# Interleaving the two batches through three layer norms and a convolution

## What is computed

```python
def _layernorm(x, axis=-1, eps=1e-05):
    m = jnp.mean(x, axis=axis, keepdims=True)
    v = jnp.var(x, axis=axis, keepdims=True)
    return (x - m) / jnp.sqrt(v + eps)
...
# fourth sublayer, with Z = _layernorm(x)
y = Z + summary
mu = jnp.mean(y, axis=-1, keepdims=True)
var = jnp.mean((y - mu) ** 2, axis=-1, keepdims=True)
x = x + (y - mu) / jnp.sqrt(var + LN_EPS) * gamma + beta
# fifth sublayer, with x = _layernorm(x)
z = x @ W_mem
z = lax.conv_general_dilated(z, conv_k, window_strides=(1,), padding=[(CONV_W - 1, 0)], ...)   # CONV_W = 4, depthwise
q = (x @ W_q).reshape(b, l, KQ, H, M, 2)
...                                    # phases, running sums, queries, gates, an output projection
```

## Time and profile before

| | us |
|---|---|
| median of 3 runs | 438.44 |
| lowest and highest run | 437.74, 439.62 |
| the profiled execution, whole | 437.43 |
| span of its trace | 435.6 |
| PE busy in the span | 395.9 |
| DVE busy in the span | 302.9 |

### The profile page before, as it was taken

How to read it: one execution, slowest core, us unless ns; L and a number is a source line. 1 busy time by engine, 2 the same in 40 slices (tenths; PEclk the granted TensorE clock), 3 DMA queues, 4 the chain that set the end, 5 groups by cost and what they waited for, 6 DMA issues and landing times.

```text
span 435.6 us, 14368 instructions
## 1 busy us (share of the span) xinstructions
PE 395.9 (91%) x6033; PEld 330.5 (76%) x6033; DVE 302.9 (70%) x676; ACT 266.9 (61%) x552; POOL 215.3 (49%) x262
## 2 busy tenths in 40 slices
PE   6978999999999999789979977799889998999997
PEld 4656767777667777678979966577768878989996
DVE  6788989988888876558798877583896668222221
ACT  2557878888888889675545513530999235445441
POOL 2468657765567663333544630510199734444540
PEclk8989999999999999999999989999999999999999
DMA  4186732622311003520000080030000291000000
GB/s 154 30 299 220 227 123 71 221 89 78 103 38 31 29 15 102 227 89 2 0 2 2 1 320 13 10 124 2 1 2 2 78 391 71 2 1 2 0 2 24
DMA packets 10831, 34.77 MB, mean 80 GB/s; under 512 B 2192, under 2 KB 7312, under 8 KB 8976
## 3 DMA queue, kind: packets, MB, share of 16 engines
q1 hardware_dynamic: 10480, 33.08, 21.7%
q10 hardware_dynamic: 288, 0.79, 0.5%
HBM read 33.60 MB, written 0.26 MB: 78 GB/s over the span
## 4 chain that ended last, share of the span: by engine, by line
PE 63%; DVE 20%; POOL 6%; ACT 5%; issue 4%; DMA 1%; SPq 0%; DVEq 0%; POOLq 0%; ACTq 0%
PE ps L1599 9%; PE ps L1089 8%; PE ps L1554 8%; PE ps L1075 6%; PE ps L405 3%; PE ps L1586 3%; PE ps L1569 3%; PE ps L466 2%; PE ps L815 2%; PE ps L797 2%; PE ps L391 2%; PE ps L351 2%; PE ps L756 2%; PE ps L763 2%; ACT sb_arena L1520 1%
## 5 line engine op out<-in xcount | busy, mean ns | idle before, releaser
L1520 ACT ACTIVATE sb_arena<-ps 128x1024 f32<-128x1024 f32 x128 | 123.4, 1019 | 22.5 <-PE ps L1586 22.4
L1599 PE MATMUL ps<-sb_arena 128*25 128x128 f32 (+1 forms) x2048 | 69.0, 274 | 0.9 <-issue 0.8
L1599 PEld LDWEIGHTS ps<-sb_arena 128*25 128x25 f32 (+1 forms) x2048 | 50.4, 97 | 8.3 <-issue 1.2
L1554 PE MATMUL ps<-sb_halves 128*128 128x512 f32 x192 | 54.3, 419 | 1.7 <-DVE sb_arena L1342 1.0
L1121 POOL TENSOR_TENSOR sb_halves<-sb_big,sb_halves 128x704 fp32r<-128x704 f32 x20 | 33.7, 1687 | 38.7 <-ACT sb_halves L1115 38.7
L495 POOL TENSOR_TENSOR sb_halves<-sb_big,sb_halves 128x256 fp32r<-128x256 f32 x32 | 23.7, 760 | 45.8 <-ACT sb_halves L479 45.8
L1187 DVE SCALAR_TENSOR_TENSOR sb_arena<-ps,sb_w_q,sb_arena 128x176 f32<-128x176 f32 x40 | 16.0, 401 | 42.7 <-ACT sb_arena L1139 42.5
L1554 PEld LDWEIGHTS ps<-sb_halves 128*128 128x128 f32 x192 | 34.4, 192 | 14.4 <-issue 6.2
L1089 PE MATMUL ps<-sb_halves 128*128 128x352 f32 x240 | 42.9, 332 | 2.0 <-POOL sb_halves L1121 2.0
L1414 POOL TENSOR_TENSOR sb_big<-sb_arena 128x256 f32<-128x256 f32 x31 | 19.0, 613 | 49.4 <-DVE sb_arena L1303 49.4
L1089 PEld LDWEIGHTS ps<-sb_halves 128*128 128x128 f32 x240 | 39.1, 189 | 3.3 <-DVE sb_arena L1187 1.7
(11 more groups left out here) (223 smaller groups left out, 862.4 us busy)
## 6 DMA issues: line engine op xcount, KB each, us to landing
sb_arena<-in_ctx SPq DMA_DIRECT2D x32, 128.0 KB, 2.1
sb_mid<-in_w_down SPq DMA_DIRECT2D x1, 3584.0 KB, 12.3
sb_big<-in_w_gu SPq DMA_DIRECT2D x1, 3520.0 KB, 11.9
sb_mid<-in_w_ffn SPq DMA_DIRECT2D x3, 768.0 KB, 4.5
sb_big<-in_w_gu SPq DMA_DIRECT2D x1, 2112.0 KB, 7.7
sb_big<-in_w_q SPq DMA_DIRECT2D x2, 1024.0 KB, 5.9
sb_big<-in_w_k SPq DMA_DIRECT2D x2, 1024.0 KB, 5.2
sb_big<-in_w_v SPq DMA_DIRECT2D x2, 1024.0 KB, 5.6
```

What stands on the lines that cost most here:

```text
L1520: nc.scalar.activation(probs[:, n % P_SLOTS].rearrange("p a g n -> p a (g n)"), ps[:, bank:bank + 2], ACT.Exp, scale=XD ** -0.5).then_inc( ...
L1554: i = T.matmul(ps[:, 7], ctx_half[:, t % 2, c, kt], wkv_half[:, d, kt], start=(n + kt == 0), stop=(n == 2 and kt == KT - 1))
L1599: i = T.matmul(ps[32 * gg:32 * gg + m, 6, j * P:(j + 1) * P], v_sb[:, t % V_SLOTS, 4 * gg + j, head], probs[:, n % P_SLOTS, a, gg], start= ...
```

## The change

The first two norms are fused: since the second norm subtracts the mean anyway, `sum_in` multiplies x by the first norm's 1/sqrt and adds the summary, in one instruction, without subtracting the first mean. The order on DVE is then written out with batch 0 ahead of batch 1, through the three norms, and the order in which ACT makes the six reciprocal roots follows it (`CHAIN`). Each batch is transposed by itself, batch 0 into bank 0 and batch 1 into bank 3, and copied by itself (`take`). PE begins the convolution of batch 0 as soon as its half of `xnT` is there, and transposes batch 1 after six of batch 0's eight matmuls. POOL adds beta after `sum_in` and no longer after the first normalisation. The matmuls on constants ahead of the transposes are 58 instead of 75. Counts that semaphores have reached are adapted.

```diff
-        WARM = {0: 20, 1: 24, 2: 24, 5: 75, 6: 24}
+        CHAIN = (("summary", 0), ("summary2", 0), ("summary", 1), ("phase", 0), ("summary2", 1), ("phase", 1))
+
+        WARM = {0: 20, 1: 24, 2: 24, 5: 58, 6: 24}
...
+        def chained(name, b):
+            return B * LN_OF["summary"] + CHAIN.index((name, b)) + 1
...
-            layer_norm(dve, LN_OF["summary"], add_previous)
-
-            def add_summary(b):
-                dve.wait_ge(sem("ln_normed"), B * LN_OF["summary"] + b + 1)
-                step(dve, V.tensor_tensor(xn[:, b], xn[:, b], sumo[:, b], ALU.add))
-            layer_norm(dve, LN_OF["summary2"], add_summary, xn, normed=False)
-
-            def add(b):
-
+            def stats(b, src):
+                step(dve, V.bn_stats(bn[:, b], src[:, b]))
+
+            def aggregate(b):
+                V.bn_aggr(mv[:, b], bn[:, b]).then_inc(sem("ln_stats"), 1)
+
+
+            def sum_in(b):
+                dve.wait_ge(sem("ln_rstd"), chained("summary", b))
+                V.scalar_tensor_tensor(xn[:, b], x[:, b], rstd[:, b:b + 1], sumo[:, b], ALU.mult, ALU.add
+                                       ).then_inc(sem("summary_added"), 1)
+                dve.wait_ge(sem("summary_added"), b + 1)
+
+            def weigh(b):
+                dve.wait_ge(sem("ln_stats"), chained("summary2", b))
                 step(dve, V.scalar_tensor_tensor(xn[:, b], xn[:, b], mv[:, b, 0:1], vecs[:, 1], ALU.subtract, ALU.mult))
-                dve.wait_ge(sem("ln_rstd"), B * LN_OF["summary2"] + b + 1)
+
+            def residual(b):
+                dve.wait_ge(sem("ln_rstd"), chained("summary2", b))
                 dve.wait_ge(sem("beta_added"), b + 1)
                 step(dve, V.scalar_tensor_tensor(x[:, b], xn[:, b], rstd[:, b:b + 1], x[:, b], ALU.mult, ALU.add))
-            return add
+
+            def normalise(b):
+                dve.wait_ge(sem("ln_rstd"), chained("phase", b))
+                V.tensor_scalar(xn[:, b], x[:, b], mv[:, b, 0:1], rstd[:, b:b + 1], ALU.subtract, ALU.mult
+                                ).then_inc(sem("ln_normed"), 1)
+
+            def take(b):
+                dve.wait_ge(sem("ln_transposed"), 4 + b)
+                V.tensor_copy(xnT[:, :, b, 3:], ps[:, 3 * b, 0:256].rearrange("p (k l) -> p k l", k=KT)
+                              ).then_inc(sem("xnT_ready"), 1)
+
+            add_previous(0)
+            stats(0, x)
+            aggregate(0)
+            add_previous(1)
+            stats(1, x)
+            sum_in(0)
+            stats(0, xn)
+            aggregate(0)
+            weigh(0)
+            aggregate(1)
+            residual(0)
+            stats(0, x)
+            aggregate(0)
+            sum_in(1)
+            stats(1, xn)
+            normalise(0)
+            aggregate(1)
+            weigh(1)
+            take(0)
+            residual(1)
+            stats(1, x)
+            aggregate(1)
+            normalise(1)
+            take(1)
...
-            ln_transpose(pe, LN_OF["phase"], 0)
-            pe.wait_ge(sem("xnT_ready"), 2)
+            keep_warm(WARM[LN_OF["phase"]], 0)
+
+            def turn_x(b):
+                pe.wait_ge(sem("ln_normed"), B * LN_OF["summary"] + b + 1)
+                for kt in range(KT):
+                    i = T.transpose(ps[:, 3 * b, kt * P:(kt + 1) * P], xn[:, b, kt * P:(kt + 1) * P], id32[:])
+                i.then_inc(sem("ln_transposed"), 1)
+
+            turn_x(0)
             pe.wait_ge(sem("w_cm_ready"), KT * CONV)
             for b in range(B):
 
+                pe.wait_ge(sem("xnT_ready"), 2 + b)
                 for n, (kt, w) in enumerate((kt, w) for kt in range(KT) for w in range(CONV)):
+                    if b == 0 and n == 6:
+                        turn_x(1)
                     i = T.matmul(ps[:, 1 + b, 0:288], xnT[:, kt, b, w:w + L], w_cm[:, kt, w], start=(n == 0),
                                  stop=(n == KT * CONV - 1))
...
-                pool.wait_ge(sem("ln_normed"), B * LN_OF["summary"] + b + 1)
+                pool.wait_ge(sem("summary_added"), b + 1)
                 G.tensor_tensor(x[:, b], x[:, b], vecs[:, 2], ALU.add).then_inc(sem("beta_added"), 1)
```

More of the change, by code:

```diff
@@ L361, in ln_transpose @@
             for b in range(B):
-                pe.wait_ge(sem("ln_normed"), B * (k - (k > LN_OF["summary2"])) + b + 1)
+                pe.wait_ge(sem("ln_normed"), B * (k - 2 * (k > LN_OF["summary2"])) + b + 1)
                 for kt in range(KT):
@@ L742, in scalar_summary @@
+            residual(0)
[12 more added lines that the diff above has]
+            take(1)
         def scalar_summary(act):
             nc.scalar.preload_act_table_set("natural_log_exp_and_others")
-            ln_rstd(act, LN_OF["summary"])
-            ln_rstd(act, LN_OF["summary2"])
+            for name, b in CHAIN:
+                act.wait_ge(sem("ln_stats"), chained(name, b))
+                nc.scalar.activation(lnv[:, b:b + 1], mv[:, b, 1:2], ACT.Ln, bias=1e-5).then_inc(sem("ln_log"), 1)
+                act.wait_ge(sem("ln_log"), chained(name, b))
+                nc.scalar.activation(rstd[:, b:b + 1], lnv[:, b:b + 1], ACT.Exp, scale=-0.5).then_inc(sem("ln_rstd"), 1)
@@ L842, in vector_phase @@
             V = nc.vector
-            layer_norm(dve, LN_OF["phase"], add_previous)
-            ln_copy(dve, 3, 0)
             def turn(kq, b):
@@ L941, in scalar_phase @@
         def scalar_phase(act):
-            ln_rstd(act, LN_OF["phase"])
             act.wait_ge(sem("logp_ready"), 1)
@@ L1044, in tensor_experts @@
             ln_transpose(pe, LN_OF["moe"], 0)
-            pe.wait_ge(sem("xnT_ready"), 3)
+            pe.wait_ge(sem("xnT_ready"), 4)
             pe.wait_ge(sem("w_moe"), loaded["w_moe"])
@@ L1166, in vector_experts @@
             layer_norm(dve, LN_OF["moe"], add_previous)
-            ln_copy(dve, 4, 0)
+            ln_copy(dve, 5, 0)
             split_x(dve, xe_half, 0, "xe")
```

## The result

| | before | changed |
|---|---|---|
| median of 20 runs each, us | 438.65 | 436.18 |
| lowest and highest, us | 436.94, 441.86 | 432.70, 440.47 |
| profiled execution, us | 437.43 | 436.96 |
| its span, us | 435.6 | 434.8 |

What follows compares the result with a forecast made beforehand. Bound: DVE's instruction list before PE may start the convolution. PE starts 3.37 us earlier, batch 1's transposes cost 0.31, leaving 3.06 us: profiled execution 437.43 to 434.4, median 438.44 to 435.4 us; range 434.1 to 437.0.

Steps and rivals of the forecast that it cites:

- The bound: Before the convolution: DVE's instruction list until PE may start sets the time; PE starts 3.37 us earlier.
- The list's sum: DVE's instructions up to batch 0's copy, priced one by one: 7.02 us, plus 0.08 for meeting POOL.
- The meeting with POOL: Batch 0's last normalisation runs during POOL's beta for batch 1 and loses 0.08 us; bounds with `weigh(0)` 0 to 0.57.
- Batch 1: Batch 1 is normalised at 294.11, 1.0 us before PE reaches its transposes at 295.1.
- Transposes inside the stream: Batch 1's two transposes, between PE's convolution matmuls, add 0.31 us.
- All of it passes: Behind the convolution: all 3.06 us of its earlier end reach the kernel's end.
- the give-back rival: Behind the convolution: another input holds the recurrence, gain shrinks to 1 us or less, about 437.8; chance 0.13.
- The clock: Rival at the convolution: fewer matmuls on constants let PE's clock fall; 3.4 us there lose 1.7; chance 0.06.
- the sum: Convolution ends at 300.45 instead of 303.51, 3.06 us earlier; median becomes 435.4.
- the time around the span: Execution time outside the trace's span, taken as unchanged at 1.83 us.
- the prediction's bounds: Limits for the profiled execution: 434.1 to 435.0 us around 434.4; for the median, 435.1 to 436.0.

Runs made afterwards that it cites:

- the kernel with the later beta: Changed kernel, but POOL adds batch 1's beta only after batch 0's last normalisation; DVE's first addition to convolution end took 16.25 us, against 15.75.
- the experiment that takes the cover away: Changed kernel, but batch 1 transposed after all eight of batch 0's matmuls, not six; DVE's first addition to convolution end took 16.53 us, against 15.75.
- the kernel with ACT's copies: Changed kernel with batch 0 further ahead, 50 matmuls on constants, ACT copying the transposed batches; medians 434.2 and 434.45 us, ratios 0.9873 and 0.9896 to the kernel before.

## Why the prediction was right

**The bound.** DVE's list up to the first convolution matmul was named as the bound, and shortening it moved PE's start by what it was shortened: the list up to the copy, its waits included, went from 10.20 to 6.95 us and the copy from 0.69 to 0.42, the step from the copy to PE grew by 0.11, and PE's start came 3.41 earlier. Delaying DVE by POOL's beta (16.25) moved the stage by the same half microsecond. The list's sum was 7.10 us to `take(0)` (with 0.08 for the meeting); it measured 6.95. The list took durations as if each instruction waited for the one ahead; where none does, the next starts before the end, as the combining at 293.12, 0.38 behind a normalisation that took 0.46. The other way, the step from DVE's copy to PE, taken at 0.05 from the kernel before, measured 0.16 (294.26 to 294.42), and 0.14 to 0.16 in every kernel of this study but the one before; why is open. The two misses nearly cancel, so that PE started at 7.53 us where 7.57 were forecast is in part luck.

**The meeting with POOL.** Taken at 0.08 from one row, measured 0.05: 0.46 against the 0.41 of the kernel with the later beta, where the combining behind it starts 0.33 after it instead of 0.38. A wait until POOL's recorded end (292.33 + 0.72 = 293.05) would have been 0.31; it wasn't. `weigh(0)`, for which the bounds allowed 0.20, lost nothing.

**Batch 1.** 1.0 us to spare at the transposes were forecast and 1.3 measured; the experiment that takes the cover away shows what it was worth, 0.78.

**Transposes inside the stream.** 0.31 forecast from four of them between matmuls; the chain shows 0.22 (297.57), and the convolution with them takes 8.22 instead of 8.03.

**All of it passes.** 132.09 to 132.21 us follow behind the stage in every kernel, so the give-back rival is out for the span: nothing behind the convolution hung on anything but the convolution.

**The clock.** It stayed at 1.00 in the changed kernel. The rival exists, as the run with 20 fillers shows, and its price had been put too low for one fall: 2.32 us instead of 1.7, since the lower level lasted about 7 us, in which PE was busy for 5.10, and not 3.4 as in the earlier trace rows.

**What the sum lacked.** The stage gave 3.22 us, a little more than the 3.06 of the sum, and yet the measured median, 436.18, is above the 435.4 of the forecast. Two things stand between, beside the scatter of the runs (432.70 to 440.47). The kernel before measured 438.65 over 20 runs where three had 438.44. And the time around the span, which the prediction counted as fixed (437.43 - 435.6 = 1.83), was not: over 16 runs of the kernel before it lay between 1.74 and 1.86 us, over 11 runs of the changed one between 2.09 and 2.18. So some 0.3 us of the 3.22 are given back where the trace has no rows. 3.22 - 0.33 = 2.89 us of 438.65 is a ratio of 0.9934, which lies in both measured intervals. Of the prediction's bounds, 435.0 is the meeting at 0.57 with the transposes at 0.44; for 434.1 it gives no term, the meeting at nothing making 434.3. What makes the 0.3 us around the span is open. It isn't the number of matmuls on constants (2.14 with 75, 2.20 with 40), nor the fusion (1.82) nor the order (1.76) by itself, and in the kernel with ACT's copies it is gone again (1.76 to 1.85 in 12 runs).

## What to carry to other kernels

Where two independent halves go through a chain of small dependent instructions, count the chain's instructions one by one up to the point at which the next engine may start, and put into the first half's waits only what fits there; order was worth more here than the fused instruction. Whatever filled the time of the long chain, such as matmuls that only hold the clock, must be cut to the new length, neither left as it is nor cut so far that the granted clock falls, as it did with 20. When a kernel's time scatters by more than the change is worth, read the changed stage from several profiles: it repeated to 0.01 us where whole executions differed by several. And look at the granted clock ahead of the stage before a difference is put down to a change.

## What the runs showed of the hardware beyond that

The clock's lower level lasted 3.4 us in one fall (256.8 to 260.2 in the kernel before) and 6.8 in another (290.0 to 296.9, with 20 matmuls on constants). In the first PE had been at work again for 1.3 us when the clock fell, and went on without a gap; in the second PE was still idle when it fell, until 291.22, and then worked with a gap of 0.68 us. The length of a hole did not tell by itself whether the clock fell: with 2.03 us in the stage it did not, with 2.7 us near 228 it did in seven of thirteen executions, and with 3.02 us, where the kernel before has the fall of the earlier trace rows, it did not in the run with 20 (1.00 from 252 to 264). From a combining to DVE's use of ACT's root it took 0.68 to 0.69 us in some places and 0.76 in others. The longer ones had in front of them an instruction whose own end DVE waits for; in the kernel with ACT's copies, where a combining that nobody waits for stands in between, it was 289.63 - 288.94 = 0.69 again. Whether that is the cause was not tried. And the time of an execution outside its first and last recorded instruction differed between kernels by 0.3 us, repeatably.
